# Two query maps of two neighbouring key heads in one unit of an attention loop

## The reference

```
x = rmsnorm(tokens, norm_w)
q = (x @ Wq)  -> 16 query heads of 64         (QH = 16)
kv = x @ Wkv  -> 8 key heads and 8 value heads of 64   (H = 8)
q = l2norm(q) * (q_gamma + 1) * 8 ;  k = l2norm(k) * (k_gamma + 1) * 8
q = q.reshape(b, H, g=2, n, 64)               # query heads 2h and 2h+1 belong to key head h
sim = tanh(q k^T / 50) * 50 / 8 ;  sim = where(causal, -max, sim)
attn = softmax(sim)
out[h] = sum over g, j of attn[h, g, i, j] * v[h, j]     # both maps of a key head are added
return out @ Wout
```

## Time and profile before

| | |
|---|---|
| median of 3 runs | 2039.68 us (2038.79 to 2041.76) |
| profiled execution, whole | 2037.89 us |
| its span in the trace | 2036.2 us |
| mean granted TensorE clock | 0.958 of full |
| PE busy over the span | 1841.0 us (90%) |
| DVE / ACT / POOL busy | 1184.6 / 876.8 / 473.1 us |

### The profile page before, as it was taken

The page is one execution under the profiler, slowest core; times in us unless marked ns, Lnnn a source line. Parts: engine busy times, 40 slices in busy tenths (PEclk is TensorE's granted clock), DMA queues, the critical chain, the costliest instruction groups (busy, mean ns, idle before and its releaser), DMA issues. The chain is left out here.

```text
span 2036.2 us, 31526 instructions
## 1 busy us (share of the span) xinstructions
PE 1841.0 (90%) x11768; PEld 1585.8 (78%) x11768; DVE 1184.6 (58%) x2083; ACT 876.8 (43%) x1076; POOL 473.1 (23%) x376
## 2 busy tenths in 40 slices
PE   3699999999969989998998999699999999999997
PEld 2698988988957877777787778578778787777876
DVE  6788788888865786776678676323241423414141
ACT  3655654545525764664576466122221222222221
POOL 2100000000022231221232123133433324333342
PEclk8799999999998999998999999799999999999999
DMA  8131222224001002000200100150000000000000
GB/s 168 49 128 49 96 78 90 76 99 143 22 32 63 23 15 77 24 15 9 85 23 15 56 22 22 49 223 14 8 21 0 21 0 21 21 0 21 0 11 12
DMA packets 17240, 96.81 MB, mean 48 GB/s; under 512 B 3270, under 2 KB 3398, under 8 KB 11209
## 3 DMA queue, kind: packets, MB, share of 16 engines
q1 hardware_dynamic: 17100, 94.90, 13.9%
HBM read 82.27 MB, written 24.15 MB: 52 GB/s over the span
## 5 line engine op out<-in xcount | busy, mean ns | idle before, releaser
L556 PE MATMUL conv<-w_hi,x_hi 128*128 128x368 f16 (+5 forms) x1320 | 355.8, 279 | 4.2 <-DVE planes L452 4.2
L556 PE MATMUL conv<-w_lo,x_hi 128*128 128x368 f16 (+5 forms) x1320 | 356.2, 279 | 0.0
L556 PE MATMUL conv<-w_hi,x_lo 128*128 128x368 f16 (+5 forms) x1320 | 355.0, 279 | 0.0
L818 POOL TENSOR_TENSOR probs<-probs,mask 128x512 f32<-128x512 f32 x128 | 166.8, 1303 | 444.1 <-ACT probs L892 444.1
L1310 ACT ACTIVATE raw_c<-ring,sh 128x512 f32<-128x512 f32 x128 | 88.2, 689 | 370.3 <-PE ring L1407 370.3
L1098 PE MATMUL mixed<-v,probs 128*128 128x65 f32 x1536 | 202.9, 283 | 41.5 <-DVE parts L978 41.5
L1098 PEld LDWEIGHTS mixed<-v,probs 128*128 128x128 f32 x1536 | 187.2, 197 | 56.8 <-issue 40.0
L1407 PE MATMUL ring<-ha_hi,wh 128*128 128x512 f32 x512 | 208.2, 407 | 16.9 <-POOL ha_lo L1272 16.9
L1272 POOL TENSOR_TENSOR ha_lo<-raw_c,ha_hi 128x512 fp32r<-128x512 f32 x128 | 165.0, 1289 | 210.1 <-DVE ha_hi L1322 210.1
L1407 PE MATMUL ring<-ha_lo,wh 128*128 128x512 f32 x512 | 205.4, 401 | 0.0
L1322 DVE CAST ha_hi<-raw_c 128x512 fp32r<-128x512 f32 x128 | 80.7, 631 | 212.9 <-ACT raw_c L1310 210.7
(11 more groups left out here) (148 smaller groups left out, 3563.7 us busy)
## 6 DMA issues: line engine op xcount, KB each, us to landing
xt<-x_columns_in SPq DMA_DIRECT2D x12, 1163.0 KB, 5.3
xp<-x_patches_in SPq DMA_DIRECT2D x12, 1152.0 KB, 5.2
hidden_words<-hidden_weights_in SPq DMA_DIRECT2D x8, 1408.0 KB, 8.2
words<-hidden_words SPq DMA_DIRECT2D x32, 352.0 KB, 3.1
wh<-hidden_words SPq DMA_DIRECT2D x2, 4096.0 KB, 21.1
tokens<-planes SPq DMA_DIRECT2D x4, 1024.0 KB, 3.9
lines<-tokens SPq DMA_DIRECT2D x4, 1024.0 KB, 5.4
h<-tokens SPq DMA_DIRECT2D x4, 1024.0 KB, 7.4
```

The costliest lines, as they stand in the source:

```text
L556: ins = pe.matmul(out, xs[:, c, RI - 1 - i:RI - 1 - i + NR, :, x].rearrange("p r g -> p (r g)"), w, start=(t == 0), stop=(t == len(terms) ...
L818: pool.tensor_tensor(diag, diag, both, ALU.mult).then_inc(s_mask, 1)
```

## The change

A unit now takes one map of each of two neighbouring key heads 2p and 2p+1, instead of both maps of one key head. The 64-row halves of `kt` then hold two different key heads, which is how the projection already lays them out in `raw`. So:

- the scale step multiplies queries and keys in place by one instruction of 1536 values; the tile `keys` goes;
- one bank of key transposes per tb instead of two, 4 transposes instead of 8; DVE reads this bank twice, into the even and the odd units of `kt`; makes 11 and 15 are gone from the order;
- the mask is applied by two `affine_select` instructions of 128x256 (one for each diagonal block, both maps) instead of one product of 128x512; an instruction that only bumps a semaphore (`settle`) stands ahead of them;
- the multiply behind the mix writes `o` directly in even units; only odd units add, 256 values instead of 128;
- the query weights and the gammas are permuted on the host.

```diff
-    [("make", 11), ("make", 7), ("scale", 1)],
+    [("make", 7), ("scale", 1)],
     [("make", 12)],
-    [("make", 13), ("make", 14), ("make", 15)],
+    [("make", 13), ("make", 14)],
...
                         pool.wait_ge(s_exp, g * NH + n + 1)
-                        diag = probs[:, n % 4].rearrange("p m (b i) -> p m b i", b=3)[:, :, 0:3:2]
-                        both = mask[:].rearrange("p (m b i) -> p m b i", m=1, b=1).to_broadcast([P, 2, 2, P])
-                        pool.tensor_tensor(diag, diag, both, ALU.mult).then_inc(s_mask, 1)
+                        settle(pool, s_settle)
+                        for jb in range(2):
+                            diag = probs[:, n % 4, :, 2 * jb * P:(2 * jb + 1) * P]
+                            ins = pool.affine_select(out=diag, in_=diag, compare_op=ALU.is_ge, fill=0.0, base=0,
+                                                     pattern=[[0, 2], [1, P]], channel_multiplier=-1)
+                        ins.then_inc(s_mask, 1)
...
-                        by = rn[:, tb].rearrange("p (h d) -> p h d", d=1)
-                        dve.tensor_tensor(heads[:, 0:QH], heads[:, 0:QH], by[:, 0:QH].to_broadcast([P, QH, DH]), ALU.mult)
-                        for m in range(2):
-                            ins = dve.tensor_tensor(keys[:, tb, :, m], heads[:, QH:],
-                                                    by[:, QH:].to_broadcast([P, HEADS, DH]), ALU.mult)
-                        ins.then_inc(s_qn, 1)
+                        by = rn[:, tb].rearrange("p (h d) -> p h d", d=1).to_broadcast([P, QH + HEADS, DH])
+                        dve.tensor_tensor(heads, heads, by, ALU.mult).then_inc(s_qn, 1)
...
-                        by = gamma[:, 4 * r:4 * r + 4].rearrange("p (h t) -> p h t", t=1).to_broadcast([P, 4, P])
-                        dve.tensor_tensor(kt[:, img % 2, 4 * r:4 * r + 4, P * tb:P * tb + P], bank, by,
-                                          ALU.mult).then_inc(s_emptied["keys"], 1)
+                        for m in range(2):
+                            by = gamma[:, m::2].rearrange("p (h t) -> p h t", t=1).to_broadcast([P, EB, P])
+                            ins = dve.tensor_tensor(kt[:, img % 2, m::2, P * tb:P * tb + P], bank, by, ALU.mult)
+                        ins.then_inc(s_emptied["keys"], 1)
...
-                        dve.tensor_tensor(parts[:], got[:, :, :, 0:DH], rl[:].to_broadcast([P, 2, 2, DH]),
+                        pair = o[:, img % 2, :, 2 * (hd // 2):2 * (hd // 2) + 2]
+                        dve.tensor_tensor(parts[:] if hd % 2 else pair, got[:, :, :, 0:DH], rl[:].to_broadcast([P, 2, 2, DH]),
                                           ALU.mult).then_inc(s_mixread, 1)
-                        dve.wait_ge(s_mixread, g * NH + n + 2)
-                        dve.tensor_tensor(o[:, img % 2, :, hd], parts[:, :, 0], parts[:, :, 1],
-                                          ALU.add).then_inc(s_o, 1)
+                        if hd % 2:
+                            dve.wait_ge(s_mixread, g * NH + n + 2)
+                            dve.tensor_tensor(pair, pair, parts[:], ALU.add).then_inc(s_o, 1)
...
-                                if r < 2:
-                                    c = (4 * r + e) * P
-                                    src = raw[:, tb, c:c + P]
-                                else:
-                                    src = keys[:, tb, 4 * (r - 2) + e].rearrange("p m d -> p (m d)")
-                                ins = pe.transpose(bank[:, e * P:(e + 1) * P], src, ident[:])
+                                c = (4 * r + e) * P
+                                ins = pe.transpose(bank[:, e * P:(e + 1) * P], raw[:, tb, c:c + P], ident[:])
```

More of the change, by code:

```diff
@@ L601, in first_order @@
     order += [("make", 0, j) for j in (4, 5, 6)] + [("scale", 0, 0), ("sum", 0, 1), ("root", 0, 1)]
-    order += [("make", 0, j) for j in (3, 7, 8, 9, 10, 11)] + [("scale", 0, 1)]
-    return order + [("make", 0, j) for j in (12, 13, 14, 15)]
+    order += [("make", 0, j) for j in (3, 7, 8, 9, 10)] + [("scale", 0, 1)]
+    return order + [("make", 0, j) for j in (12, 13, 14)]
 def attention_order(last):
@@ L696, in attention_stage @@
         w_hi, w_lo, hn, squares = sh.w_hi, sh.w_lo, sh.hn, sh.squares
-        mask = sb("mask", [P, P])
         w_out = sb("w_out", [P, EB, D])
@@ L702, in attention_stage @@
         raw = sb("raw", [P, 2, QK])
-        keys = sb("keys", [P, 2, HEADS, 2, DH])
         rn = sb("rn", [P, 2, QK // DH])
@@ L796, in _ @@
             pool.memset(v[:], 1.0).then_inc(s_const, 1)
[L797 to L801, removed]
             def emit(run, g):
@@ L957, in emit @@
                         heads = raw[:, tb].rearrange("p (h d) -> p h d", d=DH)
[L958 to L963 removed]
+                        by = rn[:, tb].rearrange("p (h d) -> p h d", d=1).to_broadcast([P, QH + HEADS, DH])
+                        dve.tensor_tensor(heads, heads, by, ALU.mult).then_inc(s_qn, 1)
                     elif kind == "make" and step[2] >= 8 and step[2] % 4 >= 2:
[L965 removed]
+                        img, tb = step[1], step[2] // 4 - 2
                         bank = read_out(run, g, step).rearrange("p (h t) -> p h t", t=P)
                         dve.wait_ge(s_score, image(g, img) * HEADS + 8)
[L968 to L970 removed]
+                        for m in range(2):
+                            by = gamma[:, m::2].rearrange("p (h t) -> p h t", t=1).to_broadcast([P, EB, P])
+                            ins = dve.tensor_tensor(kt[:, img % 2, m::2, P * tb:P * tb + P], bank, by, ALU.mult)
+                        ins.then_inc(s_emptied["keys"], 1)
                     elif kind == "mix":
@@ L1078, in emit @@
                             pe.wait_ge(s_emptied["queries"], image(g, img) * 4 + 4)
-                            pe.wait_ge(s_emptied["keys"], image(g, img) * 4 + 4)
+                            pe.wait_ge(s_emptied["keys"], image(g, img) * 2 + 2)
                         pe.wait_ge(s_tanh, g * NH + n + 1)
@@ L1097, in emit @@
                                     at = P * (ib + jb)
-                                    ins = pe.matmul(out, probs[:, n % 4, m, at:at + P], v[:, img % 2, jb, hd],
+                                    ins = pe.matmul(out, probs[:, n % 4, m, at:at + P], v[:, img % 2, jb, 2 * (hd // 2) + m],
                                                     start=(jb == 0), stop=(jb == ib), skip_group_check=True)
@@ L1103, in emit @@
                         bank = free_bank(run, g, step)
-                        pe.wait_ge(s_o, g * NH + 8 * img + 8)
+                        pe.wait_ge(s_o, g * (NH // 2) + 4 * img + 4)
                         rows = o[:, img % 2, b].rearrange("p h d -> p (h d)")
@@ L1517, in per_unit, with paired @@
         return np.asarray(s).reshape(KH, P).T
+    def paired(q):
+        return q.reshape(-1, HEADS // 2, 2, 2, DH).transpose(0, 1, 3, 2, 4).reshape(-1, QH * DH)
     w = lambda a: np.asarray(a)
@@ L1522 @@
         "template": w(L0_tok_template)[:, ::-1, ::-1].reshape(CHANNELS, TAPS),
-        "w_qkv": inputs_first(np.concatenate([w(L0_attn_Wq), w(L0_attn_Wkv)], axis=1), FB),
+        "w_qkv": inputs_first(np.concatenate([paired(w(L0_attn_Wq)), w(L0_attn_Wkv)], axis=1), FB),
         "w_attn_out": inputs_first(w(L0_attn_Wout), EB),
         "norm_w": w(L0_attn_norm_w).reshape(FB, P).T,
-        "q_gamma": w(L0_attn_q_gamma).reshape(HEADS, 2, DH).transpose(1, 2, 0).reshape(P, HEADS),
-        "k_gamma": np.tile(w(L0_attn_k_gamma).T, (2, 1)),
+        "q_gamma": paired(w(L0_attn_q_gamma).reshape(1, -1)).reshape(HEADS, P).T,
+        "k_gamma": np.repeat(w(L0_attn_k_gamma).reshape(HEADS // 2, P), 2, axis=0).T,
         "hidden_weights": np.concatenate(
```

## The result

The kernel after took 1981.66 us (median of 5 executions, 1978.43 to 1996.93), the kernel before on the same chip 2041.58 us (2038.79 to 2041.76). The ratio is 0.9721, 95% interval 0.9695 to 0.9747: about 57 us less, where 23 were forecast. Two further measurements of the same kernel gave 1981.38 and 1982.11 us.

A forecast was written before the change was run, and what follows sets the result against it. PE was taken to set the pace, busy 34.5 of 36.1 us per image. The terms 6.6 + 6.2 + 5.3 + 3.6 + 1.5 = 23.2 us gave a median of 2017 us, range 2010 to 2025.

The forecast's parts named there:

- Part 1: Transposes of make 11 in slot 5: 0.44 us less PE time in each of 15 images, 6.6 us, bounds 5 to 8.
- Part 2: Transposes of make 15 in slot 7: 0.3 us in 12 images, 0.86 in 3; 6.2 us, bounds 3.8 and 8.6.
- PE's wait for the read-out of the keys: Sign in attention: this wait, 4.5 us over 7 times before, should stay or grow a little.
- Part 3: Mask by selection: shorter DVE stalls beside POOL, 0.35 us in each of 15 images, 5.3 us, bounds -2 and +10.
- Part 4 and 5: Shorter scale: 3.6 us over the first images of 4 groups, 1.5 us in the very first image.
- Part 6: The rest (settle, double bank read, SyncE, last image's longer addition): 0 us, bounds -2 and 0.
- a sign of being wrong: Mixes beginning to wait for POOL would show the forecast wrong; no size given.
- The clock at 0: PE's granted clock after waits: net effect put at 0 us, bounds -5 and +7.
- Work turned into waits: Rival: PE's removed work in slots 5 and 7 becomes waits for DVE; 9 us gain, about 2031 us; chance 0.19.
- the removed work lay beside other work: Rival of no change: the removed transposes lie beside other work, so nothing is gained; chance 0.04.
- The dear selection: Rival: each 128x128 mask block costs 1.03 us, 4.1 us per unit; 34 us slower, 2074 us; chance 0.05.
- The clock's rival: Rival: stretches at 1.2 GHz behind waits go, 7 us, with 8 for the mask; about 2007 us; chance 0.12.

The follow-up runs named there:

- e4: Kernel after with the four transposes of each key bank done twice into the same bank; 1988.77 us, ratio 0.9736.
- e10: Kernel after with the eight key transposes per image back at their old places, in banks of their own; 1988.39 us, ratio 0.9744.
- e2: Kernel before with the mask by two selections and nothing else changed; 2005.91 us, ratio 0.9833.
- e3: Kernel after with the mask by one product again; 2014.35 us, ratio 0.987.
- e7: Kernel after with the scale as long as before, an extra 128x512 instruction into a spare buffer; 1986.06 us, ratio 0.9723.
- e8: Kernel after with an extra addition of 128 values behind every even unit, into a spare tile; 1982.09 us, ratio 0.9708.
- e1: Kernel after, unchanged, measured again; 1981.38 us, ratio 0.9713.
- e9: Kernel before with PE's idle time in slot 5 filled by five 128x128 identity products per image; 2037.1 us, ratio 0.9981.
- e12: Kernel after, unchanged, measured once more beside a filled variant on the same chip; 1982.11 us, ratio 0.9701.

## Why the prediction was wrong

**The bound: right.** PE sets the pace, the waits are those of the earlier trace rows, and DVE's instructions stand still beside the mask.

**Part 1 and 2, the transposes: over.** 12.8 forecast, 7.4 (e4) and 6 to 9 (e10) measured. Part 1's 0.44 us per image is nearly what e10 shows, 0.38. Part 2's 0.3 us in slot 7 isn't there by the transposes: what shortened the way to the next image's score is the addition, which the mask no longer holds up. It was the mask's gain under another name. PE's wait for the read-out of the keys, forecast to stay at 4.5 us or grow, shows it. In e2, which keeps the eight transposes, and in e3, which has four and the product, it is

```profile
PE sim L1087 <- DVE kt L972: 1.0, 1, 1.0
```

```profile
PE sim L1077 <- DVE kt L965: 7.7, 9, 1.5
```

**Part 3, the mask: this is the step that failed.** 5.3 forecast with an upper bound of 10; 34.8 (e2) and 33.0 (e3) measured. Its pieces one by one. The selection's price, 0.45 us, was near: 0.41 undisturbed. Both together 0.9: 0.77 seen. What is left of a hit, 0.3 to 0.8 us: 0.1 to 0.2 us for one instruction, 0.25 in the quoted chain, so the gain of the hit in slot 5 is over 0.8 us (PE's wait fell from 1.05 to 0.18) where 0.25 to 0.7 were forecast. The gross error is the last factor, 0.35 us per image on the ground that "not each image has a hit". In the kernel before each of the first 15 images has 4 to 7 stalled instructions among the steps of the inverse root and the additions, 3.0 to 6.0 us of stall, and the table of groups held the sum: 64 us in these lines, by mean less median. I had read single hits off a timeline and had set their frequency by judgement. In the middle image e2 gives 1.4 us, where parts 3 and 2 together had 0.35 + 0.3. With 0.45 us taken off for each microsecond at 1.2 GHz, a group's first image gives 2.0 to 2.9 us, its third 0.6 to 1.0, its last 1.7 to 2.5. Up to the last image's first score these make 26 us, and the time at 1.2 GHz, by the same price, 5 more.

**Part 4 and 5, the scale: right, as far as e7 can tell.** 3.6 + 1.5 forecast, 4 to 5 measured (e7), and the instruction takes 1.8 us where 1.75 were worked out. From the first sum to the first score of all it is 1.70 us less, 1.6 worked out.

**Part 6: right in the time.** e8, with its additions, lies 0.7 us from e1, as two measurements of one kernel do. But the mixes did begin to wait for POOL, which the prediction had named as a sign of being wrong: once, 0.5 us, in the profile after, 5 times and 2.4 us in that of e1.

**The clock at 0: probably too low.** Bounds -5 and +7; 30 us less ran at 1.2 GHz, worth up to 8 to 14 us by the estimate above, which no run confirms. e2 alone has 16 us less in the mean (162 against 178). The argument that nothing changes at the end of a group didn't hold: the images at a group's end lost 3 to 5 us each beyond the clock, and fewer pieces at 1.2 GHz fell into them (0 to 7 us in an image after, 7 to 10 before).

**The sum.** By single edits 33 to 35 for the mask, 7 for the transposes, 4 to 5 for the scale: 44 to 47 us of 57 to 60. From e2 to e1 there are 24.5 us, and the single edits account for 12 of them. The other 12 us are not placed. The time at 1.2 GHz fell too (40.9 us in e2's loop, 17 to 26 in the kernel after's three profiles), by the prices above 4 to 10 us, but part of that is in the single edits already. No run undid two of the three parts together, so that they gain more together than one by one is possible and untested.

**The rivals.** Work turned into waits only in slot 7, and that the removed work lay beside other work is refuted by the middle image. The dear selection is refuted: the 1.03 us of the program's first selection is not the price. The clock's rival was the nearest, with 2007 us, and its 8 us for part 3 were too few by the same error.

## What to carry to other kernels

Where an engine's instruction takes several times its median, take mean less median times the count from the groups before looking at single hits: that estimates the line's whole stall. If the stalled instructions lie on a chain that the bounding engine waits for, much of it may be time: here the selections took away 50 to 53 us of stall, and 33 to 35 of them were time. A GpSimd instruction that is on no path of its own can then be worth shortening; cutting it in two without shortening gave a quarter of that here (8 to 9 us of 33).

## What the runs showed of the hardware

A VectorE instruction with two inputs in SBUF that begins while a mask instruction runs on GpSimd does its work behind it, whatever the kind of that instruction: 1299 ns behind 1.27 us, 747 behind 0.73, 599 behind 0.62, 367 to 401 behind 0.41, for a Newton step that takes 183 alone. In the kernel before each such Newton step ended 0.04 to 0.05 us behind the product, and each of 50 additions, which have more to do, 0.14 to 0.15 us behind it. Of the instructions with one input the first step of the inverse root was held up too (up to 1137 ns for 180), the sum of 1536 values was not (1.74 to 1.75 us in the 5 cases of e2 that began beside a selection). It works the other way round too: in the kernel after two selections took 2.28 us instead of 0.77, beside a scale of 1.99 us.

```profile
990.28 2.28 POOL L812 TENSOR_SCALAR_AFFINE_SELECT probs<-probs 128x256 f32<-128x256 f32 x2 [3.20 <-ACT probs L888]
990.30 1.99 DVE L955 TENSOR_TENSOR raw<-raw,rn 128x1536 f32<-128x1536 f32 x1
```

The Trainium skill, SBUF — State Buffer, section "SBUF: two separate sides", has it that of VectorE and GpSimd whichever starts first holds the shared port "for the whole instruction" and the other is blocked, for a VectorE instruction with two inputs in SBUF among others; the trace agrees, with these numbers. An instruction with one of its two inputs in PSUM isn't held up in the traces here: in the kernel before 17 of the 128 multiplies of 256 values behind the mix began beside a mask product, 9 of them lay wholly inside it, and all 128 took 424 to 427 ns.

A selection's price here is 0.29 us for 128 columns, 0.41 for 256, 0.62 for 512; a product of two inputs took 0.73 and 1.27 us for 256 and 512. From these an estimate: the selection has a fixed cost of about 0.2 us and 0.8 ns per column, where the product's slope is 2.1 ns.

A stretch of 44 us at 1.2 GHz stood over the last image in three profiles (after, e1, e9) and not in the others, with the same program in e12; the last image took 38.9 us with it and 26.1 without (e12), and what sets it off wasn't found.
